# Reciprocal norms by arithmetic, the query's norm folded into the exponential, scaling shared with GpSimd, a third buffer here and there, and a new order of steps

## What is computed

```python
# full attention, per token: 16 heads x 8
Q, K, V = x @ Wq.T + bq, x @ Wk.T + bk, x @ Wv.T + bv
attn = softmax(Q @ K.T / sqrt(8)); full = (attn @ V) @ Wo.T + bo
# local part, for layer in (0, 1): 8 heads x 64, windows of 64 tokens
q, k, v = split(shift_token(x) @ wqkv)
q = q / max(norm(q), 1e-12) * q_scale          # over the 64 numbers of a head
k = k / max(norm(k), 1e-12) * k_scale
q, k = rotary_xpos(q, k)                       # multiply by tables, add rotated halves
p = softmax(where(mask, -big, 8 * q @ k.T))    # own window and the one before
x = x + (p @ v) @ wo
h = layernorm(shift_token(x)) @ w1 + b1; a, g = split(h)
x = x + (a * gelu(g)) @ w2 + b2
```

## Time and profile before

| what | before |
|---|---|
| time, median of 3 runs | 1640.23 us (1639.82 to 1640.68) |
| time of the profiled execution | 1646.02 us, of which the span of the trace is 1644.0 |
| PE busy | 1440.7 us (88%) |
| VectorE busy | 1402.0 us (85%) |
| ScalarE busy | 1438.2 us (87%) |
| GpSimd busy | 1338.4 us (81%) |
| main DMA queue | 79.97 MB, busy 22.5% of 16 engines |

### The profile page before, as it was taken

The page is one execution under the profiler, slowest core; times in us unless marked ns, Lnnn a source line. Parts: engine busy times, 40 slices in busy tenths (PEclk is TensorE's granted clock), DMA queues, the critical chain, the costliest instruction groups (busy, mean ns, idle before and its releaser), DMA issues.

```text
span 1644.0 us, 37326 instructions
## 1 busy us (share of the span) xinstructions
PE 1440.7 (88%) x13496; PEld 1008.8 (61%) x13496; DVE 1402.0 (85%) x2052; ACT 1438.2 (87%) x4432; POOL 1338.4 (81%) x713
## 2 busy tenths in 40 slices
PE   1657999999999999999999999999999999999775
PEld 1545666666666666666666666666666666666553
DVE  3969899999999899999999999999989999998251
ACT  0647999999999999999999999999999999999582
POOL 2848988899888888898888889888888899888250
PEclk9878999999999999999999999999999999999797
DMA  5112212132222212222221213222221222221110
GB/s 148 24 32 43 56 24 56 39 67 45 62 56 62 52 27 53 51 56 56 62 56 37 56 34 67 44 62 56 63 51 27 53 51 56 49 62 36 33 30 26
DMA packets 206849, 82.91 MB, mean 50 GB/s; under 512 B 143266, under 2 KB 185676, under 8 KB 206668
## 3 DMA queue, kind: packets, MB, share of 16 engines
q1 hardware_dynamic: 205372, 79.97, 22.5%
q10 hardware_dynamic: 1296, 0.56, 0.1%
HBM read 17.60 MB, written 8.39 MB: 16 GB/s over the span
## 4 chain that ended last, share of the span: by engine, by line
ACT 53%; PE 20%; issue 8%; DVE 8%; DMA 6%; POOL 4%; SPq 1%; ACTq 0%; POOLq 0%; DVEq 0%
ACT sb_pl L552 12%; ACT sb_pl L559 10%; ACT sb_pT L502 6%; ACT sb_sq L529 5%; DMA sb_hs<-sb_x 4%; ACT sb_gate L583 3%; PE banks L866 3%; ACT sb_v L502 3%; PE banks L771 2%; ACT L552 2%; ACT L583 2%; ACT sb_kT L502 2%; DVE sb_qk L699 2%; DVE sb_t L704 2%; PE banks L845 2%
## 5 line engine op out<-in xcount | busy, mean ns | idle before, releaser
L477 POOL TENSOR_TENSOR sb_qk<-sb_qk,sb_t 128x1024 f32<-128x1024 f32 x128 | 306.3, 2393 | 121.2 <-DVE sb_t L704 121.2
L483 POOL TENSOR_TENSOR sb_rn<-sb_rn,sb_half 128x16 f32<-128x16 f32 x128 | 374.5, 2926 | 10.7
L552 ACT ACTIVATE sb_pl<-banks,sb_nml 128x128 f32<-128x128 f32 x1024 | 368.1, 401 | 2.3 <-DVE sb_nml L715 1.8
L559 ACT ACTIVATE sb_pl<-sb_pl,sb_rl 128x128 f32<-128x128 f32 x1024 | 334.3, 451 | 11.2 <-DVE sb_rl L720 11.2
L472 POOL TENSOR_TENSOR sb_pr<-sb_qkvf 128x2048 f32<-128x2048 f32 x64 | 291.1, 4548 | 31.3 <-DVE sb_qkvf L662 28.7
L489 POOL TENSOR_TENSOR sb_qk<-sb_qk,sb_rn 128x1024 f32<-128x1024 f32 x128 | 243.8, 1904 | 16.6 <-POOL sb_rn L483 0.4
L552 ACT ACTIVATION_READ_ACCUMULATOR sb_pl<-banks,sb_nml 128x1 f32 x1024 | 247.2, 241 | 0.0
L715 DVE TENSOR_REDUCE sb_nml<-banks 128x4 f32<-128x512 f32 x256 | 167.3, 680 | 37.5 <-PE banks L845 37.5
L855 PE MATMUL banks<-sb_ident,sb_pl 128*128 128x128 f32 x1024 | 157.2, 282 | 38.8 <-ACT sb_pl L559 19.2
L771 PE MATMUL banks<-sb_wqh,sb_hh 128*128 128x512 f32 x384 | 171.9, 448 | 17.2 <-DVE sb_t L704 10.3
L699 DVE TENSOR_TENSOR sb_qk<-banks,sb_tab 128x1024 f32<-128x1024 f32 x128 | 155.2, 1212 | 34.8 <-ACT sb_sq L529 33.7
(11 more groups left out here) (116 smaller groups left out, 3412.9 us busy)
## 6 DMA issues: line engine op xcount, KB each, us to landing
sb_vs<-sb_v SPq DMA_DIRECT2D x224, 128.0 KB, 2.4
sb_xt<-x SPq DMA_DIRECT2D x16, 256.0 KB, 3.1
sb_hh<-sb_sh SPq DMA_DIRECT2D x32, 128.0 KB, 2.4
sb_hl<-sb_sl SPq DMA_DIRECT2D x32, 128.0 KB, 2.4
heads_scratch<-sb_ofs SPq DMA_DIRECT2D x64, 64.0 KB, 3.3
sb_hs<-sb_x SPq DMA_DIRECT2D x32, 128.0 KB, 2.3
sb_orow<-heads_scratch SPq DMA_DIRECT2D x16, 256.0 KB, 4.0
sb_ob<-x SPq DMA_DIRECT2D x16, 256.0 KB, 3.3
```

The costliest lines, as they stand in the source:

```text
L477: nc.gpsimd.tensor_tensor(qk[:, k, :], qk[:, k, :], t2[:], ALU.add).then_inc(s_add.sem, 1)
L483: nc.gpsimd.tensor_tensor(rn[:, k, :], rn[:, k, :], half[:, 0:1].to_broadcast([P, 16]), ALU.pow).then_inc(s_rn.sem, 1)
L552: last = nc.scalar.activation(pl[:, k, m, :], ps[:, m * P:(m + 1) * P], ACT.Exp, bias=nml[:, k, m:m + 1], accum_out=suml[:, k, m:m + 1])
L559: last = nc.scalar.activation(pl[:, k, m, :], pl[:, k, m, :], ACT.Copy, scale=rl[:, k, m:m + 1])
```

## The change

- `rnorm` is no longer a power per block but twelve small arithmetic operations per two blocks (128x32 numbers), each waiting for the one before on the same engine: a maximum, a start value from the bits of the number taken as an integer, and two correction steps. `ssq` and `rn` get four buffers.
- The norm of q is no longer multiplied into q: `normed` works on the half of k alone (128x512). It comes in as the `scale` operand of the exponential instead, and the row maxima are multiplied by it: `row_max` is one step for both banks, with a third small instruction that waits for the first two.
- `scale` of the odd numbers 1, 3, 5 and 7 of a unit is one GpSimd instruction on 128x512 numbers, and those with even numbers stay four ScalarE instructions each.
- `qk`, `xT`, `x1` and the scratch of the heads have three buffers; `xt`, `st` and `ob` have two. The semaphores of x's loads and of the output's stores are split by parity.
- New slots for all steps, with the same nominal period. From a unit's first projection to its `down` they span 137 instead of 108. The first units' projections stand at 26, 100, 150 and 200 (three of layer 0, then the first of layer 1), the last ones' at 1401, 1475, 1525, 1576 and 1625. The units of layer 0 and 1 have the same order within 50.
- The preparation of the weights on VectorE (`split_q`, `tables`) stands behind the first block statistics and the first `x_low`.
- The masked value is -2^80 instead of -2^124, and the program asks for less DMA scratch memory.

```diff
-PLS = 4
+PLS, RNS = 4, 4
+POOL_SCALED = (1, 3, 5, 7)
+QKB = 3
...
+FIRST_UNITS = ((0, 0), (1, 0), (2, 0), (0, 1), (1, 1))
+LAST_UNITS = ((B - 2, 0), (B - 1, 0), (B - 3, 1), (B - 2, 1), (B - 1, 1))
+FIRST_AT = (-0.4981, 0.9699, 1.9864, 2.9852, 3.9913)
+LAST_AT = (-4.9944, -3.5181, -2.5142, -1.5061, -0.5095)
...
-    "shift_x": (-4.14,), "project_qk": (0.00, 10.79, 20.70, 33.41), "square": (2.72, 13.64, 27.89, 36.99),
+    "shift_x": (50.81,), "project_qk": (51.08, 62.22, 71.83, 86.19), "square": (53.92, 65.15, 79.61, 88.34),
...
-    "scale": (32.88, 35.19, 50.04, 54.40, 59.46, 59.80, 69.09, 70.25),
-    "probs_t": (33.62, 39.26, 54.13, 56.62, 60.49, 66.18, 70.60, 71.08),
+    "scale": (96.14, 100.59, 108.01, 112.92, 118.25, 126.46, 137.85, 139.20),
+    "probs_t": (99.63, 106.69, 115.83, 115.84, 121.64, 134.40, 140.03, 140.16),
...
-    "o_copy": (50.43, 65.48, 71.13, 75.97), "out_local": (78.57,), "x2": (80.56,), "shift_x2": (81.66,), "center": (85.17,),
+    "o_copy": (121.44, 124.56, 143.87, 145.38), "out_local": (148.92,), "x2": (153.31,), "shift_x2": (158.09,),
+    "center": (159.37,), "center_sq": (161.28,), "variance": (163.35,), "veps": (164.42,), "rstd2": (165.74,),
...
-    "split_w3": (-480.06,), "split_q": (-92.09, -13.09), "tables": (-18.77, 60.23), "fold": (27.68,), "gain": (79.90,),
+    "split_w3": (-43.86,), "split_q": (6.64, 44.24), "tables": (21.59, 29.85), "fold": (60.52,), "gain": (89.86,),
...
+            def newton(op, x, y):
+                tt, ts = nc.gpsimd.tensor_tensor, nc.gpsimd.tensor_scalar
+                hx_, hxy_, aux_ = hx[:, :, :], hxy[:, :, :], aux[:, :, :]
+                if op == 0:
+                    return ts(hx_, x, TINY, 0.5, ALU.max, ALU.mult)
+                if op == 1:
+                    return ts(y.bitcast(I32), hx_.bitcast(I32), -0.5, SEED, ALU.mult, ALU.add)
+                if op in (2, 8):
+                    return tt(hxy_, hx_, y, ALU.mult)
+                if op in (3, 9):
+                    return tt(aux_, hxy_, y, ALU.mult)
+                if op == 4:
+                    return ts(hxy_, aux_, 2.0, -5.0 / 3.0, ALU.mult, ALU.add)
+                if op == 5:
+                    return tt(aux_, hxy_, hxy_, ALU.mult)
+                if op == 6:
+                    return ts(aux_, aux_, 0.375, 5.0 / 6.0, ALU.mult, ALU.add)
+                if op == 10:
+                    return ts(aux_, aux_, -1.0, 1.5, ALU.mult, ALU.add)
+                return tt(y, y, aux_, ALU.mult)
...
                 if kind == "rnorm":
-                    nc.gpsimd.tensor_scalar(rn[:, k, :], ssq[:, k, :], TINY, None, ALU.max).then_inc(s_rn.sem, 1)
-                    pool.wait_ge(s_rn.sem, s_rn.at(step, step, 1))
-                    nc.gpsimd.tensor_tensor(rn[:, k, :], rn[:, k, :], half[:, 0:1].to_broadcast([P, 16]), ALU.pow).then_inc(s_rn.sem, 1)
+                    for op in range(12):
+                        if op:
+                            pool.wait_ge(s_rn.sem, s_rn.at(step, step, op))
+                        newton(op, x, y).then_inc(s_rn.sem, 1)
                 if kind == "normed":
-                    nc.gpsimd.tensor_tensor(q3, q3, rn[:, k, :, None].to_broadcast([P, 16, LD]), ALU.mult).then_inc(s_nrm.sem, 1)
+                    nc.gpsimd.tensor_tensor(k3, k3, rn[:, TURN[step] % RNS, LH:2 * LH, None].to_broadcast([P, LH, LD]), ALU.mult).then_inc(s_nrm.sem, 1)
+                if kind == "scale" and n in POOL_SCALED:
+                    nc.gpsimd.tensor_tensor(pl[:, k, :, :], pl[:, k, :, :], rl[:, k, :, None].to_broadcast([P, 4, P]), ALU.mult).then_inc(s_scale[1].sem, 1)
...
                 if kind == "exp":
-                        last = nc.scalar.activation(pl[:, k, m, :], ps[:, m * P:(m + 1) * P], ACT.Exp,
-                                                    bias=nml[:, k, m:m + 1], accum_out=suml[:, k, m:m + 1])
+                        last = nc.scalar.activation(pl[:, k, m, :], ps[:, m * P:(m + 1) * P], ACT.Exp, bias=nml[:, k, m:m + 1],
+                                                    scale=rn[:, TURN[step] // 2 % RNS, 2 * m + n % 2:2 * m + n % 2 + 1], accum_out=suml[:, k, m:m + 1])
-                if kind == "scale":
+                if kind == "scale" and n not in POOL_SCALED:
...
                 if kind == "row_max":
-                    nc.vector.tensor_reduce(nml[:, TURN[step] % PLS, :], bank(same("scores", step, n // 2), n % 2).rearrange("p (a b) -> p a b", a=4), AX_X,
-                                            ALU.max, negate=True).then_inc(s_max.sem, 1)
+                    for h in range(2):
+                        dve.wait_ge(s_scores.sem, s_scores.at(same("scores", step, n), step, h + 1))
+                        last = nc.vector.tensor_reduce(nml[:, k + h, :], bank(same("scores", step, n), h).rearrange("p (a b) -> p a b", a=4), AX_X, ALU.max, negate=True)
+                    last.then_inc(s_max.sem, 1)
+                    dve.wait_ge(s_rn.sem, s_rn.at(same("rnorm", step, n // 2), step))
+                    dve.wait_ge(s_max.sem, s_max.at(step, step, 1))
+                    nc.vector.tensor_tensor(nml[:, k:k + 2, :], nml[:, k:k + 2, :], rn[:, TURN[step] % RNS, 0:LH].rearrange("p (a h) -> p h a", h=2),
+                                            ALU.mult).then_inc(s_max.sem, 1)
```

More of the change, by code:

```diff
@@ L60 @@
 }
 FIRST_SLOTS = {
-    "x1": (109.14,), "x1_split": (125.41,), "x1_low": (127.21,),
+    "x1": (190.93,), "x1_split": (194.16,), "x1_low": (198.83,),
 }
[L64 to L69, removed]
+IN_SLOTS = {
+    "load": (-94.34,), "stats": (-85.35,), "rstd1": (-52.78,), "norm": (-39.56,), "norm_t": (-1.18,), "x_split": (10.59,),
+    "x_low": (12.04,),
+}
@@ L82, with unit_at, heads_at, stand @@
          "center": 1, "variance": 1, "spread": 1, "up": 2, "down": 1, "attn_t": 1, "final": 1}
+def unit_at(s, l):
+    if (s, l) in FIRST_UNITS:
+        return FIRST_AT[FIRST_UNITS.index((s, l))]
+    if (s, l) in LAST_UNITS:
+        return 2 * B + LAST_AT[LAST_UNITS.index((s, l))]
+    return 2 * s + (2 if l else -1)
+def heads_at(s):
+    if s in FIRST_HEADS:
+        n = FIRST_HEADS.index(s)
+        return HEADS_AT[n], HEADS_SCALE[n]
+    if s in LAST_HEADS:
+        n = len(FIRST_HEADS) + LAST_HEADS.index(s)
+        return 2 * B + HEADS_AT[n], HEADS_SCALE[n]
+    return 2 * s - 1, 1.0
 def all_steps():
     at = {}
+    def stand(table, s, l, place, scale=1.0):
+        for kind, slots in table.items():
+            for n, slot in enumerate(slots):
+                at[kind, s, l, n] = place * PERIOD + slot * scale
     for s in range(B):
-        place = 2 * PERIOD * s
-        edges = (FIRST_LATER if s == 0 else 0.0, -LAST_SOONER if s == B - 1 else 0.0)
         for l in range(DEPTH):
[L91 to L101, removed]
+            stand(UNIT_SLOTS, s, l, unit_at(s, l))
+            stand((FIRST_SLOTS, LAST_SLOTS)[l], s, l, unit_at(s, l))
+        stand(IN_SLOTS, s, 0, unit_at(s, 0))
+        stand(HEADS_SLOTS, s, 0, *heads_at(s))
+        stand(OUT_SLOTS, s, 0, unit_at(s, 1))
+    stand(PREP_SLOTS, 0, 0, 0.0)
     return sorted(at, key=lambda step: (at[step], step))
@@ L247, in build @@
         of = full_ps[:, H * H:H * H + H * D].rearrange("p (q d) -> p q d", q=H)
[L248 removed]
+        scratch = nc.dram_tensor("heads_scratch", (3, H, S, D), F32, kind="Internal").ap()
         scale_rows = gate[:, 0, 0:DEPTH * 2 * LD].rearrange("p (l k d) -> p l k d", l=DEPTH, k=2)
@@ L264, in build @@
         s_bias = signal("biases_added", "biases", 2)
-        s_load = signal("x_loaded", "load", unit=16)
+        s_load = [signal(f"x_loaded_{k}", "load", unit=16, only=lambda step, k=k: step[1] % 2 == k) for k in range(2)]
         s_bn = signal("block_stats", "stats")
@@ L299, in build @@
         s_scores = signal("scores_filled", "scores", 2)
-        s_max = signal("row_maxima", "row_max")
+        s_max = signal("row_maxima", "row_max", 2)
         s_exp = signal("exponentials", "exp")
         s_rec = signal("row_reciprocals", "row_recip")
-        s_scale = signal("probs_scaled", "scale")
+        s_scale = [signal(f"probs_scaled_{name}", "scale", only=lambda step, k=k: (step[3] in POOL_SCALED) == bool(k)) for k, name in enumerate(("act", "pool"))]
         s_pt = signal("probs_transposed", "probs_t")
@@ L326, in build @@
         s_x1l = signal("x1_low", "x1_low")
-        s_again = signal("x_again_loaded", "x_again", unit=16)
+        s_again = [signal(f"x_again_loaded_{k}", "x_again", unit=16, only=lambda step, k=k: step[1] % 2 == k) for k in range(2)]
         s_res = signal("result_done", "result")
@@ L330, in build @@
         s_add_x = signal("x_added", "add_x")
-        s_store = signal("output_stored", "store", unit=16)
+        s_store = [signal(f"output_stored_{k}", "store", unit=16, only=lambda step, k=k: step[1] % 2 == k) for k in range(2)]
         ring = Ring()
@@ L795, in _ @@
                     for b in range(NB):
-                        last = nc.tensor.transpose(ps[:, b * P:(b + 1) * P], xt[:, b, :], ident[:])
```

(1 more changed line is left out.)

157 lines of the change are left out of this document (86 added, 71 removed).

## The result

The changed kernel takes 1697.66 us (median of 4 runs, 1695.26 to 1701.9) against 1640.45 for the kernel before: a ratio of 1.034, interval 1.031 to 1.038. The forecast was 1580. The profiled execution took 1701.9 us, its span is 1699.9.

What follows compares the result with a forecast made beforehand. ScalarE was taken to set the period (89.6 of 93.7 us per two units), three engines close behind. From 1646.0, minus 35 (period), 22 (start) and 3 (end) gave 1586, as a median 1580 us; range 1545 to 1625.

Steps and rivals of the forecast that it cites:

- VectorE's added work: At row_max, 8 small multiplications per two units, each 0.15 us plus 0.10 wait: 2.0 us, VectorE at 88.6.
- The period: Steady stretch: two units take 91.2 us, 2.5 less than before, 14 times: 35 us saved, bounds 14 and 66.
- Three engines within 2.5 us of each other: Steady stretch: reason given against less idle time than before, when choosing 91.2 us between 89.0 and 92.7.
- ScalarE: Per two units: scalings leaving save 9.3 us, the exponentials' second operand costs 5.8; 89.6 falls to 86.1 us.
- GpSimd: Per two units: powers and half of normed leave, scalings and 48 small operations come; 83.4 falls to 75.6, busy near 72.
- The slower rival: Odd scalings queue late on GpSimd and stop TensorE's transposes: period 98.2, median 1693 us; chance 0.13, including costlier small operations.
- The start: First units: SP's loads set the start, 10 us sooner, plus 12 from closer units: 22 us saved, bounds 8 and 30.
- The end: Last units: 7 us from an earlier last unit, less 4 for crowding: net 3 us saved, bounds +20 and -10.

Runs made afterwards that it cites:

- the 1540 us version: The changed kernel with the norm of q multiplied in by GpSimd again, so no small VectorE multiplication and no second exponential operand; 1539.92 us, ratio 0.938 to the kernel before.

## Why the prediction was wrong

**The step that failed** is VectorE's added work: "8 x 0.25 = 2.0 us; bounds 0.6 and 3". The instruction took 1.02 us and not 0.15, 8.2 us per period, almost three times the upper bound. It made VectorE the fullest engine by far, with 94.3 us instead of 88.6, and the period 98.6 instead of 91.2. These 7.4 us, 14 times, are 104 of the 118 us by which the forecast was missed. The row for a small instruction was one with a single input in SBUF, and the row for the wait one whose first input is in PSUM. The price depends on where the inputs lie and on what GpSimd does, and I had compared only sizes. The rule stands in the Trainium skill, in "SBUF — State Buffer", section "Who interferes with whom": a VectorE instruction with two SBUF inputs contends with a GpSimd instruction that reads SBUF, and the port pair that they share is an exclusive lock. For GpSimd's sums and products the traces agree, within 0.03 us. For its powers they don't: these read SBUF as well, and none of the 76 above held VectorE, so here the measurement decides. GpSimd is busy for 81 per cent of the span, and most of its powers leave with the change, so the bound from above should have been a whole GpSimd addition, 2.4 us or more. With one like that for each of 8, VectorE's bound would have been 106 us, and the slower side would have had far more than 0.13.

**The period.** "I take 91.2" had a mechanism and a size. Without any multiplication and with the second operand the period is 91.8, the time 1588; an unheld multiplication adds 11 us to the 1540 us version. So without the hold the time would have been some 1599 us, an estimate that adds the two, and the forecast of 1580 some 20 us low. But the reasoning that ScalarE at 86.1 no longer matters was wrong: taking its 5.9 us away from an engine that was not the fullest gave 3.6 us of period. "Three engines within 2.5 us of each other" stood there as a reason against, and was worth more than I gave it.

**ScalarE** was right. Exponentials of the changed kernel, start to start 613.92 to 614.35, 0.43 us against 0.34 before:

```profile
613.92 0.45 ACT L612 ACTIVATE sb_pl<-banks,sb_nml,sb_rn 128x128 f32<-128x128 f32 x1
614.26 0.20 ACT L612 ACTIVATION_READ_ACCUMULATOR sb_pl<-banks,sb_nml,sb_rn 128x1 f32 x1
614.35 0.45 ACT L612 ACTIVATE sb_pl<-banks,sb_nml,sb_rn 128x128 f32<-128x128 f32 x1
```

The read of the row sum hides none of it, and busy time came to 87.3 us per period (86.1 forecast).

**GpSimd** was right. The twelve operations start at 606.02 and the next instruction at 610.03, 4.0 us (12 x 0.34 = 4.1 forecast); busy time is 71.2 (near 72).

```profile
606.02 0.32 POOL L493 TENSOR_SCALAR sb_hx<-sb_ssq 128x32 f32<-128x32 f32 x1
...
610.03 1.04 POOL L545 TENSOR_TENSOR sb_qk<-sb_qk,sb_rn 128x512 f32<-128x512 f32 x1
```

**The slower rival** gave 1693 us and the measurement 1698, which is a coincidence. Its mechanism, transposes waiting for GpSimd's scaling, is absent. TensorE's waits in the changed kernel from 424 to 801 us:

```profile
PE banks L935 <- ACT sb_pl L612: 3.4, 4, 0.8
...
PE banks L924 <- POOL sb_pl L549: 0.2, 1, 0.2
```

It appears where GpSimd has no air, in the run with sharing alone.

**The start** was put at 22 us. SyncE's issues and VectorE's rows, to be read against the earlier trace rows:

```profile
29.13 0.53 SPq L440 DMA_DIRECT2D sb_hh<-sb_sh  x1
...
90.72 0.82 SPq L440 DMA_DIRECT2D sb_hh<-sb_sh  x1
...
128.31 0.73 SPq L467 DMA_DIRECT2D sb_hs<-sb_x  x1
```

```profile
27.24 0.87 DVE L708 BATCH_NORM_STATS2 sb_st<-sb_xt 128x6 f32<-128x128 f32 x4 [8.54 <-DMA sb_xt<-x]
...
28.44 0.66 DVE L718 TENSOR_TENSOR sb_sl<-banks,sb_sh 128x512 fp32r<-128x512 f32 x1
...
33.31 6.68 DVE L690 TENSOR_TENSOR sb_tab<-sb_tab,sb_gate 128x1024 f32<-128x1024 f32 x2
```

The first shift comes 5.4 us sooner, not 10. I had left out that the second sequence's statistics stand ahead of the low part in VectorE's order, and their x, loaded behind all weights, lands at 27.24. The second unit starts 23 us sooner. But the first unit's x2 is shifted at 128.3, 16 us later than before; that units which start closer share the engines would explain it and was not tested. The table multiplications, with two SBUF inputs as well, take 6.68 us for two, 2.9 before. The third unit's x2 is shifted at 248.6 in the changed kernel and at 238.7 in the 1540 us version, before at 236.5, so at that point nothing of the 22 us is there.

**The end** was put at 3 us. The 10 us measured lie within its bounds, but they are against a regular end, not against that of the kernel before.

## What to carry to other kernels

Price a small VectorE instruction by where its inputs lie: with both in SBUF and GpSimd at work, its upper bound is GpSimd's longest sum or product (its powers did not hold it), and one input in PSUM takes that away (11 us instead of 81 for the same 128 instructions). Ask of each part of a change which engine it loads before asking which it relieves: here the sharing of the scaling loses 108 us alone and is worth 131 in the new order, and the folding that came with it cost 158. With three engines about equally full, taking 5.9 us of work off one of them shortened the period by 3.6, though the other two stayed within 1.3 us of where they were.

## What the runs showed that I had not expected

- A VectorE product of 128x8 with two SBUF inputs: 0.17 to 2.43 us, mean 1.02, ending within 0.03 us of GpSimd's sum or product; with one input in PSUM 0.166 to 0.169.
- A power on GpSimd (128x16 in 2.92 us, 128x4 in 1.01) did not hold such a product in any of the 76 cases in the kernel before with the added product.
- It works in the other direction too. In the start of the changed kernel GpSimd's product of 128x4, elsewhere 0.20 us, starts at 30.94 and takes 0.88: it ends 0.06 us after VectorE's subtraction with two SBUF inputs (L673, from 30.00 to 31.76), under which it started. No experiment was made on this direction.

```profile
30.00 1.76 DVE L673 TENSOR_TENSOR sb_wql<-sb_pl,sb_wqh 128x1536 fp32r<-128x1536 f32 x1
...
30.94 0.88 POOL L521 TENSOR_TENSOR sb_nmr<-sb_nmr,sb_rs 128x4 f32<-128x4 f32 x1
```

- The new order leaves the fullest engine 2.4 us idle in 88.2, the old one 4.1 in 93.7.
